# A 7x7 attention-like convolution before attention and experts: nine of the last row block's 28 products on GpSimd

## The chip, the cores and the metric

The kernel runs on one core of a Trainium2 chip. A core has TensorE (PE), VectorE (DVE), ScalarE (ACT), GpSimd (POOL) and SyncE (SP), which issues the transfers. Each engine takes its instructions in order, and engines wait for each other by semaphores. The metric is the device time of one execution in microseconds (us). A difference of about 0.2% (3.9 us here) is what a measurement of this kernel can tell from no change.

## What is computed

The whole reference is a convolution block, then attention over 3136 tokens, then a mixture of experts, each added to its input. Only the convolution is touched. Its end, cut to what matters (B = 4 images, 32 channels in the hidden part, 8 heads of 8 channels, 56 x 56 pixels, 49 offsets):

```
diff = jnp.stack([x1 - x2p[:, :, dy:dy + H, dx:dx + W] for dy, dx in OFFS], axis=2)
y = jax.nn.relu(_bn(diff, ...));  y = jnp.einsum('bkln,ok->boln', y, cw1)
y = jax.nn.relu(_bn(y, ...))
logits = jnp.einsum('bkln,ok->boln', y, cw2) + cw2_b[None, :, None, None]
wgt = jax.nn.softmax(logits, axis=2)
for k, (dy, dx) in enumerate(OFFS):
    patch = x3p[:, :, dy:dy + H, dx:dx + W].reshape(B, HN, SP, H, W)
    out = out + patch * wgt[:, :, k][:, :, None]
```

## The kernel before

`conv_prepare` computes x1, x2 and x3. `conv_main` does the rest in 7 row blocks (chunks) of 8 rows, 448 pixels each. The 49 offsets of a chunk are taken in 14 steps (7 rows of the kernel window, each as 4 and then 3 offsets), so there are N = 98 steps, counted through all chunks. The last chunk is the steps s = 84 to 97. In a step the 128 partitions hold 4 images x 4 offsets x 8 heads.

A step goes through these stages: `sub` on GpSimd (differences, L368), a relu on ScalarE (L456), four groups of hidden matmuls (L538) into the four PSUM banks `ps_hid`, a relu (L463), logit matmuls (L553), logits to the SBUF ring `lg` of 18 steps (L468) and a running maximum on VectorE (L401). When a chunk's 14 steps are through, the maximum is completed in `topb` (L409), and `shift` on GpSimd subtracts it (L375). Then follow, a step each:

- `exp_wide` on ScalarE (L475): the exponentials of step s, into the one PSUM bank `ps_ev`;
- `exp_ext` on ScalarE (L480): the same exponentials into the last 56 columns of the product buffer `prod`, for the softmax's denominator;
- `product(s, hs)` on VectorE (L424), hs = 0 and 1, each one half of the 8 channels of a head: exponentials (PSUM) times a shifted window of x3 (SBUF, `win`), 128 x 1792 elements, into half hs of `prod`. I call it a half-product;
- `sums(s, hs)` on TensorE (L581): four matmuls of 504 columns in four column groups, which add up over all steps of the chunk in `ps_acc`.

There is one product buffer per half: `product(s, hs)` waits for `sums(s-1, hs)`, `exp_ext(s)` for `sums(s-1, 1)`, and `exp_wide(s)` for `product(s-1, 1)`, since it overwrites `ps_ev`.

Every engine runs the same loop over turns T, a program written out in order: `hidden` is at turn T = s, shift at s + 17, exp and product at s + 18. So at T = 98 the front half of the pipeline is through, and from T = 102 to 115 only the last chunk's products and sums are left. At T = 102 to 104 the close of the chunk before (chunk 5) is mixed in: `sums_out` (ACT, L488 and L489), reciprocal (DVE, L439), `place` (ACT, L499), `widen` (PE, L569), `widened` (ACT, L506), the multiplication of `cout` (DVE, L433), and the stores on SP. At the very end the same close follows for chunk 6 alone.

GpSimd has two more instructions after its loop: it adds the block's input x to the first six chunks of the result in `front` (L386, 128 x 2688 elements each), once SP has fetched both. All engines meet at a barrier at the end of `conv_main`, ahead of the attention.

```
if s >= 1:
    v.wait_ge(acc_done, 2 * (s - 1) + hs + 1)       # product, L419
act.wait_ge(prod_done, 2 * s)                        # exp_wide, L474
act.wait_ge(acc_done, 2 * s)                         # exp_ext, L479
```

## Time and profile before

| | us |
|---|---|
| median of 3 runs | 1970.3 |
| lowest, highest | 1969.34, 1971.79 |
| the profiled execution | 1970.36 |
| its span in the trace | 1968.2 |
| PE busy | 1712.3 (87%) |
| DVE busy | 1227.8 (62%) |
| ACT busy | 1160.4 (59%) |
| POOL busy | 665.3 (34%) |

The profiled execution is at the median (0.06 us over it), and 2.2 us of it lie outside the span. The busy shares are means over stages that are limited by different engines, so they say little of one stage. The convolution's main part lies between about 60 and 637 us of the span; the last chunk's products between 559.5 and 624.1 us. A row of a timeline has the start in us, the duration in us of the merged instructions, the engine, the line, and in brackets the idle time before it and what ended it. TensorE shows each fp32 matmul as two instructions, so one `sums` is x8 there. "PEclk" is the clock granted to TensorE as a share of 2.4 GHz: 0.50 is 1.2 GHz.

### The profile page before, as it was taken

To read this page: it belongs to the slowest core of one execution; us is meant where nothing else is said; L and a number is where in the kernel's file an instruction comes from. 1 tells how busy PE (TensorE), PEld (TensorE's weight loads), DVE (VectorE), ACT (ScalarE), POOL (GpSimd) and SP (SyncE) were. 2 spreads that over 40 slices of the span, in tenths; PEclk is the share of its full clock that TensorE was granted. 3 is DMA by queue.
4 is the path that set the end of the run, shared out by engine and by line. 5 is a ranking of instruction groups with operands and counts; after the bars stand their busy time and mean duration, and the time that the engine had idled before them with its cause. 6 is when DMAs were issued, how large, how long until landed. Compare 5 with 4: busy or idle time off the path is not lost. (4 is left out here: it accounts for less than half of the span.)

```text
span 1968.2 us, 33809 instructions
## 1 busy us (share of the span) xinstructions
PE 1712.3 (87%) x13187; PEld 626.5 (32%) x13187; DVE 1227.8 (62%) x1835; ACT 1160.4 (59%) x1568; POOL 665.3 (34%) x392
## 2 busy tenths in 40 slices
PE   4468778778765789999999999999987999999998
PEld 1011111111111434433443343444344334433333
DVE  3249999999996566666666666666365345453433
ACT  2799989999922434444444444444454546566564
POOL 0798978988641310000000000000030113332222
PEclk9799999999987679999999999999986999999999
DMA  2121211211230210000000000100021000010000
GB/s 97 82 103 44 83 43 42 83 54 34 81 129 21 98 34 15 15 15 15 14 13 15 13 15 15 48 15 16 15 84 33 8 5 8 8 40 8 7 10 9
DMA packets 27711, 73.27 MB, mean 37 GB/s; under 512 B 6968, under 2 KB 16184, under 8 KB 26160
## 3 DMA queue, kind: packets, MB, share of 16 engines
q1 hardware_dynamic: 27424, 70.31, 11.2%
q8 instruction: 101, 1.65, 0.4%
q10 hardware_dynamic: 144, 0.96, 0.1%
q14 instruction: 42, 0.34, 0.1%
HBM read 47.84 MB, written 13.62 MB: 31 GB/s over the span
## 5 line engine op out<-in xcount | busy, mean ns | idle before, releaser
L1142 ACT ACTIVATE at_prob<-at_ps_s 128x896 f32<-128x896 f32 x336 | 304.8, 917 | 361.0 <-PE at_ps_s L1029 353.0
L1292 DVE TENSOR_REDUCE at_mpart<-at_ps_m 128x1 f32<-128x384 f32 (+3 forms) x800 | 396.4, 556 | 119.3 <-PE at_ps_m L1007 90.0
L424 DVE TENSOR_TENSOR cm_prod<-cm_ps_ev,win 128x1792 f32<-128x1792 f32 x196 | 388.3, 2018 | 13.4 <-ACT cm_ps_ev L475 9.5
L368 POOL TENSOR_TENSOR cm_diff<-front 128x1792 f32<-128x1792 f32 x98 | 320.6, 3275 | 69.1 <-POOLq L113 39.0
L1814 ACT ACTIVATE ge_hid<-ge_ps,ffn 128x448 f32<-128x448 f32 x448 | 249.3, 633 | 123.0 <-PE ge_ps L1681 123.0
L1045 PE MATMUL at_ps_a<-at_prob,win 128*64 128x448 f32 x1344 | 295.8, 554 | 0.0
L581 PE MATMUL cm_ps_acc<-cm_prod,cst 128*32 128x504 f32 x1568 | 218.9, 631 | 76.0 <-DVE cm_prod L424 45.8
L1029 PE MATMUL at_ps_s<-vh,front 64*128 64x448 f16 x1344 | 252.1, 352 | 2.9 <-DMA vl<-at_mrow 2.9
L1029 PE MATMUL at_ps_s<-vl,front 64*128 64x448 f16 x1344 | 251.2, 351 | 0.0
L946 POOL TENSOR_TENSOR attn<-attn 64x448 f32<-64x448 f32 x28 | 31.6, 1129 | 528.7 <-DMA attn<-attn 528.7
L1658 PE MATMUL ge_ps<-ge_hid,ffn 128*64 128x448 f32 x896 | 194.3, 555 | 0.5 <-DVE ge_part L1992 0.4
L1007 PE MATMUL at_ps_m<-front,vh 64*128 64x384 f16 (+1 forms) x800 | 166.7, 337 | 17.7 <-DVE at_mpart L1292 16.6
L463 ACT ACTIVATE cm_hid<-cm_ps_hid,cst 128x1792 f32<-128x1792 f32 x98 | 171.0, 1745 | 0.0
L1681 PE MATMUL ge_ps<-attn,w1h 128*128 128x448 f16 (+1 forms) x448 | 161.0, 359 | 0.0
L1681 PE MATMUL ge_ps<-attn,w1l 128*128 128x448 f16 (+1 forms) x448 | 159.9, 357 | 0.0
L456 ACT ACTIVATE cm_diff<-cm_diff 128x1792 f32<-128x1792 f32 x98 | 147.9, 1510 | 13.8 <-POOL cm_diff L368 13.8
L1985 DVE COPY ge_wide<-ge_ps 128x448 f32<-128x448 f32 x112 | 69.9, 624 | 135.3 <-PE ge_ps L1671 134.9
L538 PE MATMUL cm_ps_hid<-cm_diff,cst 32*32 32x448 f32 x2744 | 102.5, 554 | 55.6 <-ACT cm_hid L463 37.8
L375 POOL TENSOR_TENSOR cm_lg<-cm_lg,cm_topb 128x448 f32<-128x448 f32 x98 | 112.0, 1151 | 47.9 <-DVE cm_topb L409 47.9
L1992 DVE SCALAR_TENSOR_TENSOR ge_part<-ge_ps,ffn,ge_wide 128x448 f32<-128x448 f32 x112 | 76.4, 682 | 77.4 <-PE ge_ps L1658 75.8
L553 PE MATMUL cm_ps_lg<-cm_hid,cst 128*32 128x448 f32 x784 | 94.8, 554 | 23.9 <-ACT cm_rden L506 7.9
L1007 PEld LDWEIGHTS at_ps_m<-front,vh 64*128 64x128 f16 (+1 forms) x800 | 61.1, 94 | 171.0 <-DVE at_mpart L1292 131.0
(221 smaller groups left out, 1871.4 us busy)
## 6 DMA issues: line engine op xcount, KB each, us to landing
win<-x_dram SPq DMA_DIRECT2D x28, 868.0 KB
at_rden<-rden_dram SPq DMA_DIRECT2D x28, 224.0 KB, 3.3
x_dram<-win SPq DMA_DIRECT2D x4, 962.0 KB
conv_out<-cm_cout SPq DMA_DIRECT2D x28, 112.0 KB, 4.0
win<-x SPq DMA_DIRECT2D x2, 1568.0 KB, 12.2
t_dram<-front SPq DMA_DIRECT2D x2, 1568.0 KB, 6.8
attn<-attn SPq DMA_DIRECT2D x28, 112.0 KB, 2.2
front<-t_dram SPq DMA_DIRECT2D x2, 1568.0 KB, 9.0
```

The lines of the kernel that those rows point to most:

```text
L368: pool.tensor_tensor(diff[:, s % ND, 0:n, :].rearrange("p n (r c) -> p n r c", c=W), a.rearrange("p n (r c) -> p n r c", c=W), b, ALU.subt ...
L424: v.tensor_tensor(prod[:, hs, :, 0:CH].rearrange("p s (r c) -> p s r c", c=W), ev.rearrange("p s (r c) -> p s r c", c=W), wv, ALU.mult).th ...
L463: act.activation(hid[0:n, s % 2, :, :], ps_hid[0:n, :, 0:CH], ACT.Relu, bias=vec("t2")[0:n]).then_inc(hrelu_done, 1)
L581: ins = pe.matmul(ps_acc[32 * r:32 * r + 32, hs, 0:CH + EXT], mat("tap_in", 32), prod[:, hs, r, :], start=(k == 0), stop=(k == STEPS - 1), ...
L1007: ins = pe.matmul(ps_m[0:w, j % RB, 0:KEYS], queries, xs[rows, b, kb * KEYS:(kb + 1) * KEYS], start=True, stop=True, tile_position=(64 * h ...
L1029: ins = pe.matmul(bank[:, a, :], xs[rows, m, at:at + TT], half[rows, m, columns_of(k)], start=(part + h == 0), stop=(part + h == 2), tile_ ...
L1045: ins = pe.matmul(ps_a[64 * a:64 * a + 64, 0:CH], xT[:, m // 2, t, 64 * i:64 * i + 64], prob_of(s)[:, a, :], start=(s == 0), stop=(s + a = ...
L1142: act.activation(prob_of(s)[0:w, 0:a, :], ps_s[0:w, (s + 1 - par) % 2, 0:a, 0:CH], ACT.Exp).then_inc(exp_done, 1)
L1292: v.tensor_reduce(mpart[0:w, a, part:part + 1], ps_m[0:w, j % RB, 0:rough_columns(e)], AX.X, ALU.max).then_inc(rough_max, 1)
L1658: ins = pe.matmul(out_bank(b, k, ep)[64 * a:64 * a + 64, 0:CH], mat("w2", n, C), hid[:, j % NHB, :], start=(h == 0), stop=(h == 1), tile_p ...
L1681: ins = pe.matmul(hidden_bank(j)[:, 0:CH], w[:, n * 128:(n + 1) * 128], own16[b // 2][:, b % 2, columns_of(k)], start=(h == 0), stop=(h == 1))
L1814: act.activation(hid[:, j % NHB, :], hidden_bank(j)[:, 0:CH], ACT.Gelu, bias=mat("b1", n, 1)).then_inc(gelu_done, 1)
```

## The change

Only the last chunk (steps D0 = 84 to 97) is different; the wait conditions of the steps before are the same as they were.

1. Of the 28 half-products every third one (index 1, 4, ..., 25) is made by GpSimd: (84,1), (86,0), (87,1), (89,0), (90,1), (92,0), (93,1), (95,0), (96,1). VectorE keeps 19.
2. GpSimd can't read the PSUM bank, so ScalarE writes the exponentials of these nine steps a second time, in place over the logits in `lg` (a third activation of 128 x 448, after `exp_ext`; semaphore `flat_ev_done`).
3. `exp_wide` writes to the four banks of `ps_hid` in turn, and waits for the products of step s - 4 in place of s - 1.
4. The buffer `diff`, free by then, becomes a second pair of product buffers, for the even steps. `product(s, hs)` waits for `sums(s-2, hs)`, `exp_ext(s)` for `sums(s-2, 1)`.
5. In GpSimd's program the half-product of step s stands behind the shift of step s + 6 (`SHIFTS_AHEAD`).

```diff
+        def by_pool(s, hs):
+            return s >= D0 and (2 * (s - D0) + hs) % 3 == 1
...
+        def halves_of(s):
+            return spare if s >= D0 and (s - D0) % 2 == 0 else prod
+        def wide_ev(s):
+            return ps_hid[:, s % B, 0:CH] if s >= D0 else ps_ev[:, 0:CH]
+        def halves_free(eng, s, hs):
+            if s == D0:
+                eng.wait_ge(hid_done, N)
+            elif s > D0:
+                eng.wait_ge(acc_done, 2 * (s - 2) + hs + 1)
+            elif s >= 1:
+                eng.wait_ge(acc_done, 2 * (s - 1) + hs + 1)
...
+                def product(s, hs):
+                    c = s // STEPS
+                    pool.wait_ge(win_in[c % 2], 64 * (c // 2 + 1))
+                    pool.wait_ge(flat_ev_done, pool_halves(s, hs))
+                    halves_free(pool, s, hs)
+                    ev = lg[:, s % RING, :].unsqueeze(1).broadcast_to([128, 4, CH])
+                    pool.tensor_tensor(halves_of(s)[:, hs, :, 0:CH].rearrange("p s (r c) -> p s r c", c=W),
+                                       ev.rearrange("p s (r c) -> p s r c", c=W), window_of(s, hs),
+                                       ALU.mult).then_inc(pool_prod_done, 1)
...
                 def exp_wide(s):
                     act.wait_ge(shift_done, s + 1)
-                    if s >= 1:
+                    if s >= D0 + B:
+                        act.wait_ge(prod_done, vector_halves(s - B, 1))
+                    elif 1 <= s < D0:
                         act.wait_ge(prod_done, 2 * s)
...
                 def exp_ext(s):
...
+                    halves_free(act, s, 1)
...
+                    if by_pool(s, 0) or by_pool(s, 1):
+                        act.wait_ge(ext_done, s + 1)
+                        act.activation(lg[:, s % RING, :], lg[:, s % RING, :], ACT.Exp).then_inc(flat_ev_done, 1)
```

GpSimd's program from the last chunk's shifts to its end, before (the names are output<-inputs, `cm_lg` the ring, `front` the result):

```order
L375 TENSOR_TENSOR cm_lg<-cm_lg,cm_topb 128x448 x5
L375 TENSOR_TENSOR cm_lg<-cm_lg,cm_topb 128x448 [waits cm_top_done]
L375 TENSOR_TENSOR cm_lg<-cm_lg,cm_topb 128x448 x13
L386 TENSOR_TENSOR front<-front,win 128x2688 [waits tres_in0]
L386 TENSOR_TENSOR front<-front,win 128x2688 [waits tres_in1]
```

And the beginning of the same stretch now (L418 is the shift, L427 the new half-product, `cm_diff` the second pair of buffers):

```order
L418 TENSOR_TENSOR cm_lg<-cm_lg,cm_topb 128x448 [waits cm_top_done]
L418 TENSOR_TENSOR cm_lg<-cm_lg,cm_topb 128x448 x6
L427 TENSOR_TENSOR cm_diff<-cm_lg,win 128x4x448 [waits cm_hid_done,cm_flat_ev_done,cm_win_in0]
L418 TENSOR_TENSOR cm_lg<-cm_lg,cm_topb 128x448 x2
L427 TENSOR_TENSOR cm_diff<-cm_lg,win 128x4x448 [waits cm_acc_done,cm_flat_ev_done,cm_win_in0]
L418 TENSOR_TENSOR cm_lg<-cm_lg,cm_topb 128x448
L427 TENSOR_TENSOR cm_prod<-cm_lg,win 128x4x448 [waits cm_acc_done,cm_flat_ev_done,cm_win_in0]
L418 TENSOR_TENSOR cm_lg<-cm_lg,cm_topb 128x448 x2
```

The first half-product stands behind seven of the last chunk's 14 shifts, the other seven shifts lie between the first five half-products, and the two additions of L386 (now L442) stand behind all nine.

TensorE at turns 102 and 103 (`sums(84, 0)`, `sums(84, 1)`, then `widen` for chunk 5), now:

```order
L642 MATMUL cm_ps_acc<-cm_diff,cst 32x504 [waits cm_prod_done,cm_ext_done,cm_acc_out]
L642 MATMUL cm_ps_acc<-cm_diff,cst 32x504 x3
L642 MATMUL cm_ps_acc<-cm_diff,cst 32x504 [waits cm_pool_prod_done]
L627 MATMUL cm_ps_lg<-cm_rden_d,cst 128x448 [waits cm_rden_placed,cm_run_done]
L642 MATMUL cm_ps_acc<-cm_prod,cst 32x504 [waits cm_prod_done,cm_ext_done,cm_wide_out]
```

The order is the one of before, but the second `sums` waits for GpSimd's first half-product, and chunk 5's `widen` is queued behind it.

ScalarE at the same turns, now (L531 `exp_wide`, L535 `exp_ext`, L540 the new activation, L546 and L547 `sums_out`, L557 `place`, L564 `widened`):

```order
L531 ACTIVATE cm_ps_hid<-cm_lg 128x448 [waits cm_shift_done]
L535 ACTIVATE cm_diff<-cm_lg 128x8x56 [waits cm_hid_done]
L540 ACTIVATE cm_lg<-cm_lg 128x448 [waits cm_ext_done]
L546 COPY cm_rden_q<-cm_ps_acc 128x112 [waits cm_out_sent,cm_acc_done]
L547 COPY cm_cout<-cm_ps_acc 128x896
L531 ACTIVATE cm_ps_hid<-cm_lg 128x448 [waits cm_shift_done]
L557 COPY cm_rden_d<-cm_rden_q 32x112 [waits cm_wide_done,cm_rden_done]
L557 COPY cm_rden_d<-cm_rden_q 32x112 x3
L535 ACTIVATE cm_prod<-cm_lg 128x8x56 [waits cm_acc_done]
L564 COPY cm_rden<-cm_ps_lg 128x448 [waits cm_out_done,cm_wide_done]
```

The exponentials of step 86, the next that GpSimd needs, stand behind `widened`, which waits for `widen` on TensorE.

## Rows read from the trace of the kernel before

**Rows 1.** Windows, all engines: span, busy time (x instructions), PEclk, DMA share, GB/s.

```profile
500.00:550.00 50.00, 38.92 (x482) 8.41 (x474) 47.81 (x33) 39.19 (x46) 26.44 (x15) 1.00 0.18 63
...
559.50:568.00 8.50, 5.76 (x30) 0.86 (x25) 8.46 (x5) 4.31 (x10) 8.21 (x8) 0.75 0.00 0
568.00:624.00 56.00, 34.80 (x200) 4.78 (x200) 48.58 (x26) 13.49 (x24) 11.83 (x2) 0.79 0.31 116
```

**Rows 2.** Timeline of one step of the last chunk, and the next one's second sum.

```profile
596.34 0.55 ACT L475 ACTIVATE cm_ps_ev<-cm_lg 128x448 f32<-128x448 f32 x1 [2.97 <-DVE cm_prod L424]
596.92 3.96 DVE L424 TENSOR_TENSOR cm_prod<-cm_ps_ev,win 128x1792 f32<-128x1792 f32 x2 [0.67 <-ACT cm_ps_ev L475]
598.16 0.58 ACT L480 ACTIVATE cm_prod<-cm_lg 128x448 f32<-128x448 f32 x1 [1.27 <-PE cm_ps_acc L581]
...
599.09 1.05 PE L581 MATMUL cm_ps_acc<-cm_prod,cst 128*32 128x504 f32 x8 [1.01 <-DVE cm_prod L424]
...
601.55 3.96 DVE L424 TENSOR_TENSOR cm_prod<-cm_ps_ev,win 128x1792 f32<-128x1792 f32 x2 [0.67 <-ACT cm_ps_ev L475]
...
603.72 3.75 PE L581 MATMUL cm_ps_acc<-cm_prod,cst 128*32 128x504 f32 x16 [1.12 <-DVE cm_prod L424]
```

**Rows 3.** Groups by form, GpSimd, 100 to 650 us.

```profile
L368 POOL TENSOR_TENSOR cm_diff<-front 128x1792 f32<-128x1792 f32 x43 | 159.9, 3719 | 10.5 <-PE cm_ps_hid L538 10.3
...
L375 POOL TENSOR_TENSOR cm_lg<-cm_lg,cm_topb 128x448 f32<-128x448 f32 x98 | 112.0, 1151 | 47.9 <-DVE cm_topb L409 47.9
L386 POOL TENSOR_TENSOR front<-front,win 128x2688 f32<-128x2688 f32 x2 | 11.8, 5916 | 18.1 <-DMA win<-x 18.1
```

**Rows 4.** Line L424 in the whole trace: ns min/median/max, first and last start.

```profile
L424 DVE TENSOR_TENSOR cm_prod<-cm_ps_ev,win x196: 2011/2015/2026, 135.1 to 622.0; 128x1792 f32<-128x1792 f32 x196
```

**Rows 5.** Timeline around the close of chunk 5.

```profile
552.33 9.90 POOL L375 TENSOR_TENSOR cm_lg<-cm_lg,cm_topb 128x448 f32<-128x448 f32 x9 [22.61 <-DVE cm_topb L409]
...
561.28 0.91 ACT L489 COPY cm_cout<-cm_ps_acc 128x896 f32<-128x896 f32 x1
...
565.61 1.73 PE L569 MATMUL cm_ps_lg<-cm_rden_d,cst 128*128 128x448 f32 x2 [0.21 <-ACT cm_rden_d L499]
567.37 0.53 ACT L506 COPY cm_rden<-cm_ps_lg 128x448 f32<-128x448 f32 x1 [1.31 <-PE cm_ps_lg L569]
...
569.14 3.96 DVE L424 TENSOR_TENSOR cm_prod<-cm_ps_ev,win 128x1792 f32<-128x1792 f32 x2
```

**Rows 6.** Timeline of GpSimd in steady state: how soon it starts after a release.

```profile
521.36 2.83 POOL L368 TENSOR_TENSOR cm_diff<-front 128x1344 f32<-128x1344 f32 x1 [0.27 <-PE cm_ps_hid L538]
```

**Rows 7.** Windows, TensorE alone: span, busy time (x), PEclk, DMA share, GB/s.

```profile
540.00:556.00 16.00, 9.31 (x64) 1.00 0.00 0
...
596.00:624.00 28.00, 18.41 (x100) 0.72 0.00 1
```

**Rows 8.** Timeline of the tail, from the last sum to the attention's first instruction.

```profile
624.08 1.05 PE L581 MATMUL cm_ps_acc<-cm_prod,cst 128*32 128x504 f32 x8 [0.79 <-DVE cm_prod L424]
...
630.87 1.09 DVE L433 TENSOR_TENSOR cm_cout<-cm_cout,cm_rden 128x896 f32<-128x896 f32 x1 [3.73 <-ACT cm_rden L506]
...
637.44 0.14 POOL L930 MEMSET at_mhalf<- 128x50 f32 x1 [39.76 <-POOLq L323]
```

**Rows 9.** Timeline: L433 beside GpSimd's shift, at the close of chunk 0.

```profile
212.61 1.13 POOL L375 TENSOR_TENSOR cm_lg<-cm_lg,cm_topb 128x448 f32<-128x448 f32 x1
213.01 1.69 DVE L433 TENSOR_TENSOR cm_cout<-cm_cout,cm_rden 128x896 f32<-128x896 f32 x1 [1.05 <-ACT cm_rden L506]
```

**Rows 10.** Line L433, from 560 us, then in the whole trace.

```profile
L433 DVE TENSOR_TENSOR cm_cout<-cm_cout,cm_rden x2: 1081/1087/1093, 568.0 to 630.9; 128x896 f32<-128x896 f32 x2
...
L433 DVE TENSOR_TENSOR cm_cout<-cm_cout,cm_rden x7: 1081/1673/1685, 213.0 to 630.9; 128x896 f32<-128x896 f32 x7
```

More of the change, by code:

```diff
@@ L316, in chunk_at, with pool_halves, vector_halves, window_of @@
             return c if k == 0 and 0 <= c < NCH else None
+        D0 = N - STEPS
+        SHIFTS_AHEAD = 6
+        spare = diff[:, :, :, :].rearrange("p d q n -> p (d q n)")[:, 0:2 * NQ * (CH + EXT)] \
+            .rearrange("p (h q n) -> p h q n", h=2, q=NQ)
+        def by_pool(s, hs):
+            return s >= D0 and (2 * (s - D0) + hs) % 3 == 1
+        def pool_halves(s, hs):
+            return sum(by_pool(t, h) for t in range(D0, N) for h in range(2) if (t, h) <= (s, hs))
+        def vector_halves(s, hs):
+            return 2 * s + hs + 1 - pool_halves(s, hs)
+        def halves_of(s):
[9 more added lines that the diff above has]
+                eng.wait_ge(acc_done, 2 * (s - 1) + hs + 1)
+        def window_of(s, hs):
+            c, k = divmod(s, STEPS)
+            dy, x0, _ = taps(k)
+            return win[:, c % 2, 4 * hs:4 * hs + 4, dy * WP:(dy + ROWS) * WP] \
+                .rearrange("p s (r c) -> p s r c", c=WP)[:, :, :, x0:x0 + W]
         def lane_bias(s):
@@ L376, in shift @@
                                        ALU.subtract).then_inc(shift_done, 1)
-                for T in TURNS:
+                def product(s, hs):
[7 more added lines that the diff above has]
+                                       ALU.mult).then_inc(pool_prod_done, 1)
+                for T in range(-1, N + SHIFT_D + SHIFTS_AHEAD):
                     if step_at(T, -1) is not None:
@@ L382, in _ @@
                         shift(T - SHIFT_D)
+                    for hs in range(2):
+                        if by_pool(T - SHIFT_D - SHIFTS_AHEAD, hs):
+                            product(T - SHIFT_D - SHIFTS_AHEAD, hs)
                 early = slice(0, PIX - CH)
@@ L578, in sums @@
                         pe.wait_ge(ext_done, s + 1)
-                    pe.wait_ge(prod_done, 2 * s + hs + 1)
+                    if by_pool(s, hs):
+                        pe.wait_ge(pool_prod_done, pool_halves(s, hs))
+                    else:
+                        pe.wait_ge(prod_done, vector_halves(s, hs))
                     for r in range(4):
                         ins = pe.matmul(ps_acc[32 * r:32 * r + 32, hs, 0:CH + EXT], mat("tap_in", 32),
-                                        prod[:, hs, r, :], start=(k == 0), stop=(k == STEPS - 1),
+                                        halves_of(s)[:, hs, r, :], start=(k == 0), stop=(k == STEPS - 1),
                                         tile_position=(0, 32 * r))
```

30 lines of the change are left out of this document (14 added, 16 removed).

## The prediction

> **What bounds the kernel now.** I read the windows first. While all stages run, VectorE is busy 47.8 of 50 us; in the last chunk (568 to 624 us) it is still busy 48.6 of 56, but GpSimd only 11.8 and ScalarE 13.5 [rows 1]. So this stretch is VectorE's, with holes. One step in the timeline shows the holes [rows 2]: two half-products take 3.96 us (1.98 each), then VectorE idles 0.67 us, because the exponential of the next step must wait until the bank is read. 596.92 to 601.55 is a step of 4.63 us. Fourteen steps fill 559.5 to 624.0. Nothing later in the program overlaps with them: the attention starts behind a barrier at 637.44, 12.3 us after the last sum ends at 625.13 [rows 8]. So a microsecond taken out here is one off the time, unless another engine takes VectorE's place. TensorE, which is busiest in the whole kernel, is not the limit in this stretch, but its clock is not steady: a sum (x8) took 1.05 us at 599.09 and two together 3.75 at 603.72 [rows 2], and the granted clock of 596 to 624 us is 0.72, a mix of 2.4 and 1.2 GHz [rows 7].
>
> **VectorE's part.** It keeps 19 half-products: 19 x 1.98 = 37.6 us against 28 x 1.98 = 55.4 now, 17.8 less, and the holes of 0.67 us go with the four banks. If VectorE stayed the limit, some 26 us would be gone. It doesn't stay it.
>
> **GpSimd's part.** The new instruction isn't in the trace. Nearest is the difference of L368, with the same 1792 elements, one input repeated four times and one a strided window: 3719 ns [rows 3]. Upwards, four shifts of 448 are 4 x 1.15 = 4.60 us, and L386 scaled from 2688 to 1792 elements gives 3.94 us (5916 x 1792 / 2688). I take 3.72, since the forms are alike; nothing there is quicker per element, and 3.5 is the least I allow, 0.2 us for the change of operation and of the output's pitch.
>
> The chain is followed from one half-product on GpSimd to the next. Two of them stand in every three steps, at (s,1) and (s+2,0).
>
> - (s+2,0) needs its flat exponentials. These come after `exp_ext(s+2)`, which waits for `sums(s,1)`, which waits for GpSimd's own half-product (s,1). So between the two lies: release 0.08, one sum, `exp_ext` 0.58, flat exponential 0.55 (as L475 [rows 2]), two releases of about 0.05, and GpSimd's start after a release, 0.27 at most, 0.22 taken [rows 6].
> - (s+3,1), the next one, needs only `sums(s+1,1)`, which is through long before. It starts at once.
>
> For the sum I take 1.20 us: 1.05 at 2.4 GHz, 1.87 at 1.2 GHz (half of 3.75), and about one in five of them slow. Today the last chunk gives TensorE 2.1 us of full-clock work in 4.63 us, 45%, and the clock dips. From 540 to 556 us it was busy 9.31 of 16 us, 58%, at a clock of 1.00 throughout [rows 7]. With the change there are six sums, 6.3 us, in 10 to 11 us, about 60%. So I expect dips, fewer than now. The gap is then 0.08 + 1.20 + 0.05 + 0.58 + 0.05 + 0.55 + 0.22 = 2.73 us.
>
> **The start.** GpSimd's shifts run from 552.33 at 1.10 us each (nine in 9.90 [rows 5]), so the seventh ends at 560.03. The flat exponentials of step 84 need only the shifts and are earlier. (84,1) runs 560.03 to 563.75. Its sum ends at about 565.0, and behind it stands chunk 5's `widen`, 1.75 us to 566.8, then its copy, 0.53, to 567.35 [rows 5]. This is the wait that the change adds: behind the sum wait `widen`, all of ScalarE's program from `widened` on, and VectorE's multiplication of `cout`. Then ScalarE does `exp_wide`, `exp_ext` and the flat exponential of step 86 (0.55 + 0.58 + 0.55 and the releases), and GpSimd starts (86,0) at about 569.3. Now `product(86,0)` starts at 569.14 on VectorE [rows 5]: the first two steps win nothing, and VectorE has done (85,0) and (85,1) meanwhile. The two shifts before (86,0) are hidden in this wait.
>
> **The chain from there.**
>
> - (86,0) 3.72, one shift 1.10, (87,1) 3.72: to 577.85; gap 2.73 (two shifts, 2.20, hidden in it): 580.6.
> - (89,0), a shift, (90,1): 8.54, to 589.1; gap 2.73 (a shift hidden): 591.85.
> - (92,0), (93,1): 7.44, to 599.3; gap 2.73: 602.0.
> - (95,0), (96,1): 7.44, to 609.5.
>
> VectorE has four half-products, 7.9 us, in each such round of 10.2 to 11.3 us, and ScalarE three `exp_wide`, three `exp_ext` and two flat ones, 5 us: both are off the path. After (96,1) come `sums(96,1)`, `sums(97,0)`, `sums(97,1)`: 0.08 + 3 x 1.20, to 613.1. This end was 625.13: 12.0 us earlier. At 1.05 a sum it would be 612.1; at 1.4, TensorE's present mean, some 615.5.
>
> **The tail gives part of it back.** Today the two additions of L386 lie at 584.8 and 591.8 us, where GpSimd has nothing else. Now they stand behind (96,1): 609.5 + 2 x 5.93 = 621.3. That is earlier than the barrier. But in the tail VectorE multiplies `cout` by `rden`, both in SBUF (L433). It starts 5.74 us after the last sum ends (625.13 to 630.87 [rows 8]), so at 618.9, beside the second addition. What that costs is in the trace: L433 takes 1.08 us with GpSimd idle, and 1.67 to 1.69 in the other five row blocks [rows 10]. There it starts 0.40 us after a shift of 1.13 us has begun, and ends 0.96 us after the shift's end [rows 9], about one undisturbed duration. Read so, it is held until GpSimd's instruction is over. Then it ends here at 621.3 - 0.1 + 1.1 = 622.3, against 620.0 if it were not held. From its end to the attention is 5.48 us (631.96 to 637.44 [rows 8]): the attention starts at 627.8, 9.6 us earlier than at 637.44.
>
> The Trainium skill (SBUF — State Buffer, SBUF: two separate sides) states that a VectorE instruction with two SBUF inputs and a GpSimd instruction that reads SBUF exclude each other for the whole instruction. By that rule the trace agrees, with 1.67 us for 1.08 [rows 10]; the sum by it is the one above, and without it 12 us would be won instead of 9.6.
>
> The half-products of VectorE are a different matter: they read one input from PSUM, and in 196 of them the longest took 2026 ns, the shortest 2011 [rows 4], though GpSimd was busy 26.4 of 50 us even in the window shown [rows 1], most of it with L368. So I charge nothing for both engines making products side by side.
>
> **Costed at nothing.** The second wait that now precedes each odd half-product in all chunks: each even one has two waits today, and the pairs still run at 1.98 us. `exp_wide` into other banks. The work after the barrier, which is the same. The fetch and x transfers, which are issued at about the same time as now (chunk 5's close is as late as it was).
>
> **The sum.** 1970.36 - 9.6 = 1960.8 for the profiled execution, whose time is the median's to 0.1 us. PREDICTED 1960.8 us, a span of 1958.6.
>
> **Bounds of this case.** GpSimd's half-product at 3.5 us gives 11.5 us of gain; at 3.94, eight of them on the chain make it about 2 us less, 7.7; with TensorE's sums at 1.4 to 1.45 as well, about 6. So 1958.9 to 1964.5.
>
> **Rivals.**
>
> - *L433 isn't held.* The five slow rows could be a fixed charge of 0.6 us for company. Then the tail ends with the sums: 12.0 - 0.6 to 12.0 us of gain, 1958.6. Against it: the end of L433 fits the shift's end. 10%.
> - *TensorE stays at 1.2 GHz.* Six sums of 1.87 are 11.2 us a round. Behind (s+2,0) three sums, 5.6 us, must pass before `sums(s+3,1)`, longer than a shift and a half-product. The round is then about 3.72 + 4 x 1.87 + 1.4 = 12.6, and the last sum ends near 623: 2.3 us of gain, 1968. For it: half the clock in parts of this stretch today. Against it: TensorE gets denser, not sparser. 6%.
> - *GpSimd is slower at a product.* At 4.60 us (four times L375) each, eight on the chain cost 7.9 us more: 1.7 us of gain, 1968.6. Against it: L368 has the same size. 6%.
> - *Slower than before: the two engines' half-products exclude each other.* Both read `win`. If each waits for the other, the last chunk takes 19 x 1.98 + 9 x 3.72 = 71.1 us and about 2 us of reciprocal and multiplication, against 64.5 now; that is some 9 us longer: 1979. It turns to a loss once about half of GpSimd's 33.5 us are serialised, as that takes the 9.6 us and no more. Against it: the 196 even durations [rows 4]. 3%.
>
> **How the numbers follow.** Forecast 74%; the rest 1% for a mishap on either side. Faster by over 0.2% (3.9 us, what a measurement of this kernel can tell from no change): the forecast and L433 not held, less a little for several bounds at once, 0.84. Within 0.2%: the two cases at 1968, and that little, 0.13. Slower: 0.03. The range runs from 1958.0, which takes in the rival without the hold, to 1966.0, for both bounds of the forecast together and the near half of a slow clock; it leaves the 1968s and 1979 out, some 17%.
>
> **What the profile would show.** Nine L427 of 3.7 us on GpSimd, the first at 560.0 and the last ending at about 609.5, in pairs with gaps of 2.7 us (after 563.75, 5.6 us). VectorE idle for some 11 us between its first and last product of the chunk, where it is 7 now. The clock over this stretch nearer 0.9 than 0.78. The last sum ending at about 613. The two L442 behind it, not earlier, and L487 (now L433) lasting 2 to 3.5 us. The attention's first MEMSET at about 628. I would be wrong if L427 were far from 3.7 us, if VectorE's products left 2.02 us, or if the pairs' gap were over 4 us.

## The result, and the profile of the changed kernel

| | before | changed |
|---|---|---|
| median, fastest and slowest of 4 runs each, one comparison | 1970.71 us (1969.34 to 1971.79) | 1958.91 us (1956.49 to 1959.32) |
| ratio to before | 1 | 0.9935, interval 0.9923 to 0.9948 |
| the profiled execution: time, span | 1970.36, 1968.2 us | 1958.88, 1957.1 us |

The kernel is faster, and by more than the 0.2% that a measurement can tell from no change. The gain is 11.8 us between the medians and 12.8 us by the ratio (1970.3 x 0.0065), where 9.6 was forecast; by the ratio the time is 1957.5 us, half a microsecond below the range's lower end of 1958.0. The median, 1958.91 us, and the profiled execution, 1958.88, lie 0.9 us above that end. One of e7's five executions below took 2026.2 us at a lower granted clock (0.92, the others 0.96) and is left out of its range, its median and its ratio.

The windows of the last chunk in the changed kernel, all engines (stretch, length, then busy time and instructions of PE, PEld, DVE, ACT and POOL, then granted TensorE clock, DMA share, GB/s):

```profile
559.50:568.00 8.50, 5.73 (x30) 1.15 (x30) 5.99 (x5) 4.45 (x11) 5.82 (x3) 0.79 0.00 0
568.00:612.00 44.00, 29.30 (x196) 7.77 (x192) 31.90 (x17) 16.02 (x31) 36.95 (x14) 0.81 0.39 147
```

Against [rows 1]: VectorE was busy 48.6 of 56 us and is now busy 31.9 of 44, 73%; GpSimd was busy 11.8 of 56 us and is now busy 37.0 of 44, 84%. The stretch has changed its owner, as the prediction said.

Lines L427 (GpSimd's half-products) and L477 (VectorE's, L424 before) in the whole trace, with ns as minimum, median and maximum, then the first and last start:

```profile
L427 POOL TENSOR_TENSOR cm_diff<-cm_lg,win x5: 3682/3691/3698, 559.4 to 606.2; 128x1792 f32<-128x1792 f32 x5
L427 POOL TENSOR_TENSOR cm_prod<-cm_lg,win x4: 3681/3682/3682, 573.7 to 602.6; 128x1792 f32<-128x1792 f32 x4
...
L477 DVE TENSOR_TENSOR cm_prod<-cm_ps_hid,win x10: 1961/2015/2026, 561.9 to 609.5; 128x1792 f32<-128x1792 f32 x10
...
L477 DVE TENSOR_TENSOR cm_diff<-cm_ps_hid,win x9: 2014/2015/2026, 558.2 to 603.2; 128x1792 f32<-128x1792 f32 x9
```

Nine of 3.68 to 3.70 us, against 3.72 assumed. VectorE's nineteen keep the durations of [rows 4] with GpSimd's beside them: the two engines' half-products don't exclude each other.

The timeline of GpSimd's rounds, with the sums (L642) and exponentials (L535 and L540) between them:

```profile
568.99 3.69 POOL L427 TENSOR_TENSOR cm_diff<-cm_lg,win 128x1792 f32<-128x1792 f32 x1 [3.67 <-issue]
...
577.48 1.05 PE L642 MATMUL cm_ps_acc<-cm_prod,cst 128*32 128x504 f32 x8 [0.21 <-POOL cm_prod L427]
...
578.60 0.58 ACT L535 ACTIVATE cm_prod<-cm_lg 128x448 f32<-128x448 f32 x1 [1.53 <-PE cm_ps_acc L642]
...
579.21 0.58 ACT L540 ACTIVATE cm_lg<-cm_lg 128x448 f32<-128x448 f32 x1
...
579.92 3.68 POOL L427 TENSOR_TENSOR cm_prod<-cm_lg,win 128x1792 f32<-128x1792 f32 x1 [0.28 <-issue]
...
594.48 3.68 POOL L427 TENSOR_TENSOR cm_prod<-cm_lg,win 128x1792 f32<-128x1792 f32 x1
...
594.67 3.59 PE L642 MATMUL cm_ps_acc<-cm_diff,cst 128*32 128x504 f32 x16 [3.52 <-POOL cm_diff L427]
598.00 3.17 PE L642 MATMUL cm_ps_acc<-cm_prod,cst 128*32 128x504 f32 x16
...
601.24 0.58 ACT L535 ACTIVATE cm_prod<-cm_lg 128x448 f32<-128x448 f32 x1 [1.91 <-PE cm_ps_acc L642]
...
602.56 3.68 POOL L427 TENSOR_TENSOR cm_prod<-cm_lg,win 128x1792 f32<-128x1792 f32 x1 [4.39 <-ACT cm_lg L540]
```

The first gap is the chain of the prediction, link by link: a half-product ends at 577.4, its sum at full clock, `exp_ext`, the flat exponential, and GpSimd 0.13 us later: 2.5 us. The last gap has one link more. TensorE comes late out of two slow sums (594.67, 3.59 us), so that `sums(93,0)` isn't done when GpSimd ends (93,1) at 598.16. Two sums, 3.17 us from 598.00, stand in the gap, where the first gap had one of 1.05: 4.4 us.

The tail (GpSimd's two additions are L442, VectorE's multiplication of `cout` L487, L433 before):

```profile
609.84 11.71 POOL L442 TENSOR_TENSOR front<-front,win 128x2688 f32<-128x2688 f32 x2
...
611.46 1.90 PE L642 MATMUL cm_ps_acc<-cm_prod,cst 128*32 128x504 f32 x16
...
618.29 4.21 DVE L487 TENSOR_TENSOR cm_cout<-cm_cout,cm_rden 128x896 f32<-128x896 f32 x1 [2.93 <-ACT cm_rden L564]
...
627.98 0.14 POOL L991 MEMSET at_mhalf<- 128x50 f32 x1 [6.43 <-POOLq L366]
```

The last sum ends at 613.36 instead of 625.13 [rows 8], 11.8 us earlier, and the attention starts at 627.98 instead of 637.44, 9.5 us earlier. VectorE's multiplication has become 4.21 us long, where it was 1.09.

To compare kernels, the span is cut at five places that every one of them has. M is where VectorE starts the instruction that releases GpSimd's first shift of the last chunk (the seventh write of `cm_topb`); L the end of the last sum; A the attention's first MEMSET; X the attention's first exponential of probabilities (the output `at_prob`); E the end of the span. From A to X it prepares its operands. All times are us, one profiled execution each; "cout" is the duration of the last multiplication of `cout`.

| kernel | M | L | A | M to L | L to A | M to A | A to X | X to E | span | cout |
|---|---|---|---|---|---|---|---|---|---|---|
| before | 551.64 | 625.13 | 637.44 | 73.5 | 12.3 | 85.8 | 76.2 | 1254.6 | 1968.2 | 1.09 |
| changed | 551.06 | 613.36 | 627.98 | 62.3 | 14.6 | 76.9 | 74.4 | 1254.7 | 1957.1 | 4.21 |
| e1_no_pool | 551.51 | 616.02 | 628.37 | 64.5 | 12.4 | 76.9 | 74.4 | 1254.8 | 1957.6 | 1.09 |
| e2_add_late | 550.48 | 611.40 | 624.58 | 60.9 | 13.2 | 74.1 | 74.9 | 1254.2 | 1953.7 | 1.09 |
| e3_one_bank | 555.28 | 619.45 | 633.39 | 64.2 | 13.9 | 78.1 | 74.9 | 1254.6 | 1962.9 | 3.32 |
| e4_one_pair | 552.54 | 653.99 | 665.82 | 101.5 | 11.8 | 113.3 | 73.8 | 1254.7 | 1994.3 | 1.36 |
| e5_before_again | 551.79 | 625.24 | 637.58 | 73.5 | 12.3 | 85.8 | 76.2 | 1254.3 | 1968.1 | 1.09 |
| e6_flat_apart | 550.44 | 604.34 | 619.61 | 53.9 | 15.3 | 69.2 | 76.3 | 1254.2 | 1950.1 | 4.00 |
| e7_flat_apart_split | 551.00 | 604.86 | 617.23 | 53.9 | 12.4 | 66.2 | 75.4 | 1254.3 | 1946.9 | 1.09 |
| e8_before_delay1 | 553.68 | 627.14 | 639.68 | 73.5 | 12.5 | 86.0 | 75.9 | 1254.4 | 1970.0 | 1.09 |
| e9_before_delay2 | 551.92 | 625.38 | 639.09 | 73.5 | 13.7 | 87.2 | 74.4 | 1254.7 | 1968.2 | 1.09 |
| e10_after_again | 551.19 | 613.51 | 628.11 | 62.3 | 14.6 | 76.9 | 74.4 | 1254.8 | 1957.3 | 4.21 |
| e11_split_again | 552.23 | 606.13 | 618.49 | 53.9 | 12.4 | 66.3 | 75.3 | 1254.7 | 1948.5 | 1.09 |

The first two rows say where the 11.1 us of span went: 8.9 between M and A, which is what the prediction was about; 0.6 ahead of M, where nothing was changed; and 1.8 between A and X, where nothing was changed either; from X on 0.1 is lost. Two things come out of the other rows at once. A kernel that is run again repeats its stretches to 0.1 us (the four that run before's program up to L have 73.5 from M to L; the changed kernel has 62.3, 14.6 and 74.4 twice). That doesn't hold for a kernel that was changed behind L: e2 has the changed kernel's instructions up to there, and took 60.9 us instead of 62.3. So I read nothing into a difference of less than about 1.5 us between two kernels from M to L. And M itself lies anywhere from 550.4 to 555.3 in programs that do the same work up to there: differences of medians carry that with them, differences from M to A don't.

### The profile page after: what moved, and what is told of

Same layout as the page of the kernel before. It is cut to its first block and busy times, and to the rows that moved or that the text cites. A ratio compares the mean times of both kernels' runs of the same rounds, so it can differ in the third digit from the quotient of the medians.

```text
span 1957.1 us, 33911 instructions
## 1 busy us (share of the span) xinstructions
PE 1703.6 (87%) x13187; PEld 626.5 (32%) x13187; DVE 1212.7 (62%) x1826; ACT 1164.2 (59%) x1577; POOL 698.1 (36%) x401
## 5 line engine op out<-in xcount | busy, mean ns | idle before, releaser
L477 DVE TENSOR_TENSOR cm_prod<-cm_ps_ev,win 128x1792 f32<-128x1792 f32 x168 | 332.9, 2017 | 5.2 <-ACT cm_ps_ev L531 1.3
L642 PE MATMUL cm_ps_acc<-cm_prod,cst 128*32 128x504 f32 x1456 | 197.4, 616 | 60.0 <-DVE cm_prod L477 26.8
L510 ACT ACTIVATE cm_diff<-cm_diff 128x1792 f32<-128x1792 f32 x98 | 147.8, 1509 | 13.7 <-POOL cm_diff L411 13.7
L418 POOL TENSOR_TENSOR cm_lg<-cm_lg,cm_topb 128x448 f32<-128x448 f32 x98 | 112.1, 1150 | 47.9 <-DVE cm_topb L465 47.9
L2110 POOL TENSOR_TENSOR ge_total<-ge_part 128x448 f32<-128x448 f32 x28 | 32.0, 1144 | 246.7 <-DVE ge_part L2053 246.7
```

Source lines behind the costliest of these rows:

```text
L477: v.tensor_tensor(halves_of(s)[:, hs, :, 0:CH].rearrange("p s (r c) -> p s r c", c=W), ev.rearrange("p s (r c) -> p s r c", c=W), window_o ...
L642: ins = pe.matmul(ps_acc[32 * r:32 * r + 32, hs, 0:CH + EXT], mat("tap_in", 32), halves_of(s)[:, hs, r, :], start=(k == 0), stop=(k == STE ...
```

## The experiments

Theory: the banks and the second pair of buffers let the engines overlap, GpSimd's half-products take VectorE's work over and become the limit themselves, and the hold of VectorE's multiplication gives a part back. The rivals are in the texts on record.

### GpSimd's share taken away

```diff
-            return s >= D0 and (2 * (s - D0) + hs) % 3 == 1
+            return False
```

> The changed kernel, but GpSimd makes none of the products: VectorE makes all 28, with the four banks and the two pairs of buffers kept. Theory: of the chunk's end coming 11.8 us earlier, GpSimd's nine products bring only the last 3, because its own chain sets the pace, and the hold of the multiplication in the tail takes those 3 back. VectorE then runs its products back to back from about 558.2: 28 x 1.98 = 55.4 us, the reciprocal 0.85, the multiplication 1.1 and a wait of about 0.3 for it, so the last product ends near 615.8, the last sum near 617, the additions lie in the middle again, the multiplication takes 1.09 us and the attention starts at about 629: 1 us later than in the changed kernel, 8.5 us before the kernel before; some 1961 us. Rival: it is GpSimd's share that brings the gain. Then without it the chunk is VectorE's as before and only a few us are left: 1966 or more.

Measured: 1959.92 us (1958.93 to 1960.97), ratio 0.9952 (0.9935 to 0.9968). The tail of this kernel:

```profile
614.97 1.05 PE L642 MATMUL cm_ps_acc<-cm_prod,cst 128*32 128x504 f32 x8 [0.79 <-DVE cm_prod L477]
...
621.81 1.09 DVE L487 TENSOR_TENSOR cm_cout<-cm_cout,cm_rden 128x896 f32<-128x896 f32 x1 [3.78 <-ACT cm_rden L564]
...
628.37 0.14 POOL L991 MEMSET at_mhalf<- 128x50 f32 x1 [31.82 <-POOLq L366]
```

All 28 half-products on VectorE, and the last sum ends only 2.2 us later after M (64.5 against 62.3). Here GpSimd is through with its additions early, the multiplication takes 1.09 us, and L to A is 2.2 us shorter. M to A is 76.9 both times. So by the profiles the nine half-products on GpSimd, for which the change is named, bring nothing as it stands: what they win at the last sum the hold in the tail takes back. All of the 8.9 us is had by the banks and the second pair of buffers alone. This is good to about 1.5 us only, by what was said of e2. The medians are 1.0 us apart (1959.92 and 1958.91); the ratios, 0.9952 and 0.9935, are further apart, but their intervals overlap.

Which of the two parts it is, the banks or the second pair, no run separates while VectorE makes all the products. The trace of before points at the banks: between 556 and 626 us its half-products waited 13 times, 8.8 us in all, each time for `exp_wide` (L475), which waits for the one bank, and never for a sum, which is what the second pair would free. In e1 the profile puts no idle time ahead of any of the last chunk's 28 half-products. 8.8 us is nearly all of the 9.0 us by which M to L is shorter (73.5 to 64.5).

### The hold: the second addition behind the multiplication

```diff
                     pool.wait_ge(tres_in[t], 32)
+                    if t == 1:
+                        pool.wait_ge(out_done, NCH)
```

> The changed kernel, but GpSimd's second addition also waits for the chunk's multiplication of cout on VectorE, so that it can't be under way beside it. Theory (the multiplication is held until GpSimd's instruction ends): the multiplication takes 1.09 us instead of 4.21 if the first addition is over by then (it ends near 615.7, the multiplication starts at 618.3), the stores are issued 3.1 us earlier, and the second addition ends near 625.3, just ahead of or at the barrier: the attention starts 2.3 to 3.1 us earlier. About 1956. Rival (a fixed charge for company, and the rest something else): the multiplication stays over 1.6 us or the attention starts at the same time as in the changed kernel.

Measured: 1956.95 us (1955.48 to 1958.32), ratio 0.9938 (0.9921 to 0.9955). The tail:

```profile
617.19 1.09 DVE L489 TENSOR_TENSOR cm_cout<-cm_cout,cm_rden 128x896 f32<-128x896 f32 x1 [3.78 <-ACT cm_rden L566]
...
618.43 5.84 POOL L444 TENSOR_TENSOR front<-front,win 128x2688 f32<-128x2688 f32 x1 [4.76 <-DVE cm_cout L489]
...
624.58 0.14 POOL L993 MEMSET at_mhalf<- 128x50 f32 x1 [0.31 <-POOLq L366]
```

With no instruction of GpSimd beside it, the multiplication is back at 1.09 us: the hold is shown. But the addition that was moved is now what ends last at the barrier (624.27, and the MEMSET 0.31 us later), so that L to A falls from 14.6 to 13.2 us only. M to A is 2.8 us shorter; the other 1.4 lie before the last sum, where nothing was moved: the last gap between GpSimd's pairs, 4.39 us in the changed kernel, is 2.92 here. The two sums that stand in it, `sums(93,0)` and `sums(93,1)`, took 1.88 us together and not 3.17. So this part goes with TensorE's clock.

### One bank for the exponentials

```diff
-            return ps_hid[:, s % B, 0:CH] if s >= D0 else ps_ev[:, 0:CH]
+            return ps_ev[:, 0:CH]
...
-                    if s >= D0 + B:
-                        act.wait_ge(prod_done, vector_halves(s - B, 1))
-                    elif 1 <= s < D0:
-                        act.wait_ge(prod_done, 2 * s)
+                    if s >= 1:
+                        act.wait_ge(prod_done, vector_halves(s - 1, 1))
```

> The changed kernel, but all exponentials go to the one bank ps_ev, and exp_wide(s) waits for VectorE's products of step s-1 as in the kernel before. Theory (GpSimd's chain is the limit, not VectorE): VectorE's holes of 0.67 us come back but lie beside GpSimd's products; only where exp_wide(89), (92), (95) stand ahead of the flat exponentials that GpSimd waits for do some 0.3 to 0.5 us come on the path, three or four times. The attention starts 0 to 2 us later than in the changed kernel: 1959 to 1961. Rival (the banks bring the gain, since they let VectorE run ahead): 14 holes of 0.67 us come back, 5 us or more later, 1964 or more.

Measured: 1962.88 us (1960.04 to 1966.73), ratio 0.9965 (0.9948 to 0.9982). From M to A it is 78.1, 1.2 us more than the changed kernel. Its median is 4.0 us above that of the changed kernel; its profiled execution is 5.8 us longer in the span, of which 4.2 lie ahead of M, where the two programs are the same, and that part isn't the banks'. With two pairs of buffers and GpSimd's chain as the limit, four banks are worth a microsecond or two (1.9 from M to L, of which a shorter hold gives 0.7 back), hardly more than the 1.4 us that the clock alone moved in e2.

### One pair of product buffers

```diff
-            return spare if s >= D0 and (s - D0) % 2 == 0 else prod
+            return prod
...
-            if s == D0:
-                eng.wait_ge(hid_done, N)
-            elif s > D0:
-                eng.wait_ge(acc_done, 2 * (s - 2) + hs + 1)
-            elif s >= 1:
+            if s >= 1:
                 eng.wait_ge(acc_done, 2 * (s - 1) + hs + 1)
```

> The changed kernel, but with one pair of product buffers: product(s,hs) waits for sums(s-1,hs), exp_ext(s) for sums(s-1,1), as in the kernel before. Theory: the second pair is what lets the two engines overlap. Without it VectorE can't begin (s+1,1) before GpSimd's (s,1) is summed, and GpSimd's (s+2,0) can't begin before sums(s+1,1), the exponentials and 0.2 us: 3.7 + 1.1 + 2.0 + 1.1 + 1.5 + 3.7 + 2.2 + 1.5 + 0.5 is some 17 us for three steps, against 13.9 before and 10.9 in the changed kernel. Over the chunk that is about 12 us slower than the kernel before: 1978 to 1985. Rival (buffers hardly matter, GpSimd's share brings the gain): at or under 1965.

Measured: 1997.41 us (1996.06 to 1997.55), ratio 1.0141 (1.0124 to 1.0158): slower than before by 27 us. A round of it:

```profile
575.24 3.68 POOL L423 TENSOR_TENSOR cm_prod<-cm_lg,win 128x1792 f32<-128x1792 f32 x1 [6.29 <-ACT cm_lg L536]
...
579.06 3.59 PE L638 MATMUL cm_ps_acc<-cm_prod,cst 128*32 128x504 f32 x16 [5.22 <-POOL cm_prod L423]
...
581.10 2.02 DVE L473 TENSOR_TENSOR cm_prod<-cm_ps_hid,win 128x1792 f32<-128x1792 f32 x1 [5.08 <-PE cm_ps_acc L638]
...
595.09 3.68 POOL L423 TENSOR_TENSOR cm_prod<-cm_lg,win 128x1792 f32<-128x1792 f32 x1 [5.20 <-ACT cm_lg L536]
```

Half-product, sum, half-product, one after the other: each engine waits over 5 us for the one before it, and a round of three steps takes 19.85 us (575.24 to 595.09) where the changed kernel needs 10.9 (568.99 to 579.92). The direction was expected, the size was not (1978 to 1985 us): I had a sum at a duration near the full clock, and here most take 1.8 to 1.9 us each, with TensorE granted 0.60 of its clock from 568 to 656 us. So GpSimd's share with four banks but without the second pair of buffers is a loss of 27 us, and with the pair a gain of about 12: the pair is needed for the split. Together with e1 it does not say that the pair brings anything without the split.

### The flat exponentials out of the chain

The prediction's chain says that GpSimd's pairs are kept apart by sum, `exp_ext` and flat exponential. If so, a flat exponential that stands ahead and has a buffer of its own should close the gaps. The buffers of `cm_hid` are idle in this stretch.

```diff
+        def flat_of(s):
+            n = sum(by_pool(t, 0) or by_pool(t, 1) for t in range(D0, s))
+            return hid[:, (n % 8) // 4, n % 4, :]
...
-                    ev = lg[:, s % RING, :].unsqueeze(1).broadcast_to([128, 4, CH])
+                    ev = flat_of(s).unsqueeze(1).broadcast_to([128, 4, CH])
...
-                    if by_pool(s, 0) or by_pool(s, 1):
-                        act.wait_ge(ext_done, s + 1)
-                        act.activation(lg[:, s % RING, :], lg[:, s % RING, :], ACT.Exp).then_inc(flat_ev_done, 1)
+
+                def exp_flat(s):
+                    if s < N and (by_pool(s, 0) or by_pool(s, 1)):
+                        act.wait_ge(shift_done, s + 1)
+                        if pool_halves(s, 1) > 8:
+                            act.wait_ge(pool_prod_done, pool_halves(s, 1) - 8)
+                        act.activation(flat_of(s), lg[:, s % RING, :], ACT.Exp).then_inc(flat_ev_done, 1)
...
                         exp_wide(T - SUM_D)
+                        if T - SUM_D == D0:
+                            exp_flat(D0)
+                            exp_flat(D0 + 1)
+                        if T - SUM_D >= D0:
+                            exp_flat(T - SUM_D + 2)
```

> The changed kernel, but the exponentials for GpSimd are not written over the logits after exp_ext, but to eight slots of the buffer hid, free by then, up to two steps ahead of exp_wide. They depend on the shift alone, so GpSimd's half-product (s+2,0) no longer waits for the sum of its own (s,1), exp_ext and the flat exponential. Theory (that chain sets the chunk's pace): the gaps of 2.7 to 4.4 us between GpSimd's pairs go, and it works through nine products and seven shifts in some 41 us from 559.4, to 600.5; VectorE, with 19 products, the reciprocal, the multiplication and its wait of 1.5 us, ends near 601 too. The last sum ends at 604 to 607 instead of 613.4, the two additions on GpSimd end near 612.3 and hold the multiplication until then, the attention starts at about 619: 9 us earlier than in the changed kernel, 1949 to 1951. Rival (VectorE or TensorE is just behind GpSimd): less than 3 us.

Measured: 1956.61 us (1951.89 to 1959.65), ratio 0.9935 (0.992 to 0.995); the profiled execution took 1951.89. GpSimd's stretch at the start of the last chunk:

```profile
564.66 3.70 POOL L431 TENSOR_TENSOR cm_diff<-cm_hid,win 128x1792 f32<-128x1792 f32 x1
...
566.70 2.61 DVE L491 TENSOR_TENSOR cm_cout<-cm_cout,cm_rden 128x896 f32<-128x896 f32 x1 [1.33 <-ACT cm_rden L572]
...
568.33 1.99 POOL L422 TENSOR_TENSOR cm_lg<-cm_lg,cm_topb 128x448 f32<-128x448 f32 x1
...
576.12 3.72 POOL L431 TENSOR_TENSOR cm_prod<-cm_hid,win 128x1792 f32<-128x1792 f32 x1
...
580.89 3.71 POOL L431 TENSOR_TENSOR cm_diff<-cm_hid,win 128x1792 f32<-128x1792 f32 x1
```

576.12 plus 3.72 plus a shift of about a microsecond is 580.89: no gaps. M to L falls from 62.3 to 53.9 us, the last sum ends at 604.34 (604 to 607 expected), the attention starts at 619.61 (619 expected). So the chain was the limit. The median doesn't show it: it is 2.3 us under that of the changed kernel and 5.6 over the 1949 to 1951 expected. This kernel's four times are spread over 7.8 us and can tell little; the profile was taken of the quickest of them.

### The same, with the second addition cut

The first part of the cut addition runs beside the last sums, the second behind the multiplication.

```diff
+                    cuts = [early] if t == 0 else [slice(0, 2 * CH), slice(2 * CH, PIX - CH)]
+                    for i, cut in enumerate(cuts):
+                        if i == 1:
+                            pool.wait_ge(out_done, NCH)
+                        ins = pool.tensor_tensor(tres[:, t, cut], tres[:, t, cut], xa[:, t, cut], ALU.add)
+                    ins.then_inc(early_added, 1)
```

> The kernel of e6 with the second addition cut in two: 896 columns at once, the other 1792 once VectorE has multiplied cout. Theory: the multiplication is beside no GpSimd instruction and takes 1.09 us, the rest of the addition ends before the barrier, and the attention starts 2 to 3 us earlier than in e6: about 616, 1946 to 1949. Rival (no hold, or the addition's rest is late at the barrier): as e6.

Measured: 1952.43 us (1948.64 to 1955.66), ratio 0.9914 (0.9899 to 0.993); the profiled execution took 1948.64. The median of these four is again above what was expected (1946 to 1949), and the profile that of the quickest. The tail:

```profile
610.65 1.09 DVE L495 TENSOR_TENSOR cm_cout<-cm_cout,cm_rden 128x896 f32<-128x896 f32 x1 [3.77 <-ACT cm_rden L576]
611.83 3.95 POOL L450 TENSOR_TENSOR front<-front,win 128x1792 f32<-128x1792 f32 x1 [1.86 <-DVE cm_cout L495]
...
617.23 0.14 POOL L1008 MEMSET at_mhalf<- 128x50 f32 x1 [1.46 <-POOLq L370]
```

The addition's rest ends at 615.78, 1.46 us before the MEMSET, so it is off the path; L to A is 12.4, that of a tail with no hold, where e6 had 15.3. This is what e2 had missed.

### Where the 1.8 us behind the barrier come from

From A to X the changed kernel took 74.4 us and before 76.2, with the same instructions. The windows of TensorE over this stretch (stretch, length, busy time and instructions, granted clock, DMA share, GB/s), first before, then the changed kernel:

```profile
637.40:657.40 20.00, 13.82 (x74) 0.76 0.45 184
657.40:677.40 20.00, 16.48 (x51) 0.50 0.33 80
677.40:697.40 20.00, 16.01 (x68) 0.60 0.00 1
697.40:713.60 16.20, 12.06 (x47) 0.59 0.01 1
```

```profile
628.00:648.00 20.00, 12.97 (x74) 0.83 0.45 183
648.00:668.00 20.00, 16.55 (x50) 0.51 0.33 80
668.00:688.00 20.00, 13.83 (x68) 0.81 0.00 0
688.00:702.40 14.40, 11.99 (x46) 0.55 0.01 2
```

Same instructions, but in the third window 13.83 us busy at a clock of 0.81 instead of 16.01 at 0.60. Is that the program's, or the moment's at which the stretch starts? Before was run again unchanged (e5), and twice with nothing but a useless addition behind GpSimd's last instruction before the barrier, to start the attention later. The edit (3776 columns instead of 3072 in e9):

```diff
+                pool.wait_ge(out_done, NCH)
+                late = diff[:, :, :, :].rearrange("p d q n -> p (d q n)")[:, 0:3072]
+                pool.tensor_tensor(late, late, late, ALU.add)
```

> The kernel before, unchanged, for a second profile of it. In the changed kernel's profile 1.7 us of the gain lie in the attention's preparation, between its first instruction and its first exponential (76.2 us before, 74.4 us after), where the program is the same. Theory: this is the phase of TensorE's clock, which stays at half or full rate in different places of a stretch that is only partly busy, and differs between executions of one program too; then this profile may show another length, anything from 73.8 to 76.5 us. Rival: the length belongs to the program (or to what the chunk before it leaves behind), and is 76.2 us here again within 0.2.

> The kernel before with one more GpSimd instruction at the end of conv_main, an addition of 3072 columns into a buffer that nobody reads, behind the last multiplication of cout. It ends some 6.6 us after it, so that the attention starts 1 to 2 us later and nothing else of it changes. The attention's preparation (its first instruction to its first exponential) was 76.2 us in both profiles of the kernel before, 74.4 in the changed one. Theory (TensorE's clock falls and rises at places that hang on when the stage starts, not on the program): the length changes by over 0.5 us, to anything from 73.8 to 77. Rival (it belongs to the program before): 76.2 us again within 0.2.

> As e8 with 3776 columns, some 8.2 us behind the multiplication, so that the attention starts about 3 us later than in the kernel before. Theory and rival as for e8; by the theory it differs from at least one of 76.2 us and e8 by over 0.5 us.

Measured, one execution each, beside before on the same chip: e5 1970.28 us (before there 1970.04, nine runs from 1968.72 to 1973.88), e8 1972.16 and e9 1970.37 us (before there 1971.79, nine runs from 1969.77 to 1972.25). e5 has 76.2 us again: its rival came out, and the length did not change between these two executions of one program. In e8 the addition was too short for its purpose, the tail grew by 0.2 us only, and A to X is 75.9: between what theory and rival asked for, so it decides nothing. In e9 the addition is what the attention waits for:

```profile
632.32 6.48 POOL L390 TENSOR_TENSOR cm_diff<-cm_diff 128x3776 f32<-128x3776 f32 x1 [34.49 <-DVE cm_cout L436]
...
639.09 0.14 POOL L933 MEMSET at_mhalf<- 128x50 f32 x1 [0.29 <-POOLq L323]
```

and TensorE's windows behind it are those of the changed kernel, each busy time to within 0.02 us:

```profile
639.10:659.10 20.00, 12.97 (x74) 0.83 0.39 162
659.10:679.10 20.00, 16.53 (x50) 0.51 0.33 80
679.10:699.10 20.00, 13.83 (x68) 0.81 0.00 0
699.10:713.50 14.40, 11.99 (x46) 0.55 0.01 3
```

So the program of before, started 1.4 us later after M, has the short 74.4 us, and its span is again 1968.2: the delay cost nothing. The 1.8 us, then, need no part of the change: a start moved by 1.4 us gives them, with TensorE's clock, in the one execution of e9. That GpSimd was at work until 0.29 us before A in e9 isn't the reason: it was so in e8 as well (75.9), and in e1 GpSimd had been idle for 31.82 us (74.4). Of what relation to what sets it, the runs don't tell: A lies at 639.68 in e8 (75.9), at 639.09 in e9 (74.4), at 637.44 and 637.58 in the two of before (76.2), and e6, earlier than the changed kernel by 8.4 us, has 76.3. That stays open.

### The changed kernel and the best one, side by side

> The changed kernel once more, beside e11 on one chip. Its gain to the attention's start was 9.5 us by the profile, 0.6 of that ahead of the last chunk, and the whole 11 to 12 us. Theory: what is over the 9.5 is not of the last chunk, but the front's length (the seventh maximum came between 550.4 and 555.3 us in nine profiles) and the clock in the attention's preparation; so the median lies between 1957 and 1961 and this profile has the maximum-to-attention time of the first one, 76.9 us, within 1 us. Rival: the change gives more than 11 us in the chunk itself, and the time from the maximum to the attention is under 76.

> The kernel of e7 once more, beside e10 on one chip. Theory: from the maximum to the attention 66 us, 10.7 less than the changed kernel; so its median is 8 to 11 us under that of e10, less what the front adds by chance. Rival (the gain is given back in the attention): under 4 us.

Measured in one comparison: e10 1959.46 us (1956.48 to 1959.83), ratio 0.9936 (0.9923 to 0.995); e11 1950.27 us (1948.40 to 1955.92), ratio 0.9897 (0.9883 to 0.9911). e11 is the kernel of e7 unchanged, and its profiled execution is the one at the median. M to A is 66.3 us against 76.9, 10.6 less, and the medians are 9.2 apart. This version beats both kernels: about 20 us under before. The share on GpSimd does pay in it: once its chain is broken and its addition out of the way of the multiplication, M to A is 10.6 us under e1, which does without that share.

## Why the prediction was right, and where it was not

**GpSimd becomes the limit: right.** First half-product at 559.43 (560.03 forecast), (86,0) at 568.99 (569.3), and the pairs end at 577.4, 588.35, 598.16 and 609.89 (577.85, 589.1, 599.3, 609.5). The wait behind chunk 5's `widen`, which the change adds, is where it was put; the half-products took 0.03 us less than assumed. e6, which cuts the chain, shows that it was the limit.

**The sum at 1.20 us, and the clock "nearer 0.9 than 0.78": the clock was wrong.** TensorE over 556 to 604 us, in before, the changed kernel, e1 and e6:

```profile
556.00:604.00 48.00, 29.70 (x166) 0.79 0.35 134
```

```profile
556.00:604.00 48.00, 32.46 (x194) 0.79 0.36 135
```

```profile
556.00:604.00 48.00, 28.45 (x194) 0.93 0.35 134
```

```profile
556.00:604.00 48.00, 34.73 (x242) 0.86 0.35 135
```

In the changed kernel TensorE did more in the same time and was granted the same 0.79. The kernel with the highest clock, e1, has as many instructions as the changed one, so denser use was not what raised it; the step "TensorE gets denser, so fewer dips" falls. It cost little, since the slow sums fell mostly outside the gaps: two gaps were 2.5 us (2.73 forecast), the third 4.4. The third is longer because of slow sums ahead of it: `sums(93,0)` stood in the gap as well as `sums(93,1)`, a queue on TensorE that the sum of the prediction doesn't have. My bound of 4 us for a gap was passed by one in three. VectorE was idle for 14.1 us between its first and last half-product, where 11 was forecast and before had 7.5. The last sum came 62.3 us after M, against 61.5 by the forecast (613.1 and M at 551.64): 0.8 us too little. (The 615.5 us given for sums of 1.4 us should have been about 614.5, as seven of the sums counted are 0.2 us longer; nothing was built on it.)

**The hold of VectorE's multiplication: right in kind, place and end.** It was to end when GpSimd's addition was over and its own 1.1 us done, at 622.3. It ended at 622.50, 0.95 us after the addition (621.55). It lasted 4.21 us instead of 2 to 3.5 because it started earlier: in this tail TensorE took 0.99 us for `widen`, which was 1.79 in before, so the multiplication stood ready 4.93 us after the last sum, not 5.74. A held instruction that is ready earlier is only held longer, and the end stays. e2, e7 and e11 take the company away and have 1.09 us. The Trainium skill (SBUF — State Buffer, SBUF: two separate sides) has the two exclude each other for the whole instruction, and by that rule the trace agrees: 4.21 us for 1.09 here, and 2.61 beside a half-product in e6.

**The attention's start: right for the most part by its own steps.** 627.98 against 627.8. Of the 9.46 us, 0.6 came from M, which was 0.6 us earlier by chance, so that the change itself gave 8.9 where 9.6 was forecast: the 0.8 us of the sums, less 0.1.

**"Costed at nothing: the work after the barrier, which is the same": this step failed.** The work is the same, and it took 1.8 us less, since TensorE's clock dips elsewhere in it. With the 0.6 us ahead of M it is the difference between 8.9 and the span's 11.1. That the clock could do this was to be seen: by [rows 7] it moves between 1.00 and 0.72 within 60 us. A stretch of 76 us behind a barrier, whose start I was about to move, is where that should have been given a price on both sides. From the 13 profiles it would have been 73.8 to 76.3 us from A to X, and 550.4 to 555.3 for M. The range reached down to 1958.0 for the case without the hold alone and left nothing for either; the ratio puts the time at 1957.5. Not all of the miss is found in the profile. It shows a gain of 11.5 us, 11.1 in the span and 0.4 outside it, and the ratio says 12.8; for the other 1.3 us no trace shows a place.

**The rivals.** Products that exclude each other: refuted by L477 and L427. GpSimd at 4.6 us a product: refuted, 3.69. TensorE at 1.2 GHz throughout: refuted as a state of the whole stretch; its slow sums fell in one gap of three. No hold: refuted by e2 and e7; its time, 1958.6, is close to the measured one for another reason, which a reader who looks at the time alone would not see.

**What the prediction left out.** It followed the change as a whole and never priced its parts against each other. The banks and the second pair alone (e1) should have been followed through the same tail: VectorE at 28 half-products is hardly slower there than GpSimd's chain (64.5 us from M to L against 62.3), and has no hold behind it. The holes of 0.67 us that the prediction read off [rows 2], 13 and 8.8 us in all, come to nearly what e1 gained up to the last sum.

## What to carry to other kernels

Before work is split between two engines, free the buffers over which they take turns, and measure that alone: here the banks and the second pair without the split had, by the profiles, the whole gain of the change, and the split without the second pair was a loss of 27 us. An engine that takes over work drags its other work later, so follow that to the next barrier, and look there for an instruction of VectorE with both inputs in SBUF, which it would hold; if there is one, cut the late work so that one part runs before it and one behind. Compare variants from one marker to the next, and give a stage behind a barrier a spread of its own where the granted clock in it isn't steady.

## What the runs showed of the hardware that I had not expected

- **A delay that costs nothing.** A start of the attention's preparation 1.4 us later after M left the span at 1968.2 us: the preparation took 74.4 us instead of 76.2, with TensorE granted 0.81 instead of 0.60 in its third 20 us. Over all runs this stretch of unchanged instructions took 73.8 to 76.3 us.
- **The hold works in the other direction too.** In e6 the shift that GpSimd had next, behind the half-product that held VectorE's multiplication, took 1.99 us where the group's mean is 1.15 [rows 3]: it began at 568.33 and ended at 570.32, 1.01 us after the multiplication (569.31). The same shift took 1.99 us in e7 and e11 too, and ended 1.0 us after the multiplication in each. This is read from the times alone.
- **More work, same clock.** 32.46 us busy of 48 at 0.79 in the changed kernel, 29.70 at 0.79 in before, 28.45 at 0.93 in e1.
